# A two-layer attention and expert kernel: second route stage and second-layer attention in one stage, first stacks loaded earlier, fewer scatters between the splits

## What is computed

```
x  = x + attn0(xn) + experts0(xn)            # layer 0, xn = layernorm(x)
xn = layernorm(x)                            # layer 1
x  = x + attn1(xn) + experts1(xn)

experts1(xn):
    h = rmsnorm(xn)
    scores = softmax(h @ gate_w.T)           # 32 experts, the best 4 of each token
    w = top4 / sum(top4)
    routed: each expert takes at most 512 rows (C = 2*N/E), later ones are dropped
    shared = silu(h @ sg) * (h @ su) @ sd
    return xn + routed + shared
```

## Time and profile before

| | us |
|---|---|
| median of three runs | 1288.99 (1284.65 to 1291.62) |
| the profiled execution | 1279.91 |
| its span | 1278.1 |
| route stage of layer 1, TensorE's first matmul to its last one's end | 894.12 to 951.85 |
| attention of layer 1, TensorE's first matmul | 969.31 |
| experts of layer 1, first load | 1069.83 |

### The profile page before, as it was taken

One profiled execution on the slowest core, in us unless ns is written; L12 is line 12 of the kernel. 1 busy time (PEld: TensorE's weight loads), 2 busy tenths in 40 slices (PEclk: granted clock), 3 DMA queues, 4 the chain that ended last, 5 costly groups with the idle time before them and its releaser, 6 DMA issues. The chain is left out here.

```text
span 1278.1 us, 20689 instructions
## 1 busy us (share of the span) xinstructions
PE 1119.2 (88%) x5586; PEld 839.3 (66%) x5586; DVE 801.9 (63%) x2224; ACT 524.2 (41%) x1423; POOL 548.8 (43%) x528
## 2 busy tenths in 40 slices
PE   5659999999987999778888999995976997999981
PEld 5436667777776888555555777785544674888861
DVE  5758787666403555379999777625834664666648
ACT  2226766555502444345555555603112331444420
POOL 0656776655200000066565655404276441555540
PEclk9779999999998999989999999998997997999985
DMA  9644442222237666432222222102557932555557
GB/s 330 248 146 164 164 144 86 76 71 72 117 139 187 182 184 182 135 100 71 79 75 71 75 75 76 28 1 78 228 201 212 297 126 61 167 165 166 164 165 246
DMA packets 118684, 177.53 MB, mean 139 GB/s; under 512 B 17231, under 2 KB 86958, under 8 KB 118046
## 3 DMA queue, kind: packets, MB, share of 16 engines
q1 hardware_dynamic: 88910, 123.45, 31.0%
q0 software_dynamic: 13808, 38.19, 8.8%
q10 hardware_dynamic: 15856, 14.56, 3.3%
HBM read 103.95 MB, written 72.19 MB: 138 GB/s over the span
## 5 line engine op out<-in xcount | busy, mean ns | idle before, releaser
L907 POOL TENSOR_TENSOR parts<-wq,parts 128x256 fp32r<-128x256 f32 x64 | 48.8, 762 | 373.9 <-ACT parts L1154 373.9
L1306 PE MATMUL bank<-big_a,probsT 128*128 x760 | 202.1, 361 | 0.3 <-DVE probsT L1386 0.2
L1163 ACT ACTIVATE probs<-bank,negmax 128x256 f32<-128x256 f32 (+3 forms) x256 | 134.7, 536 | 120.1 <-DVE negmax L1078 117.9
L970 PE MATMUL bank<-kT,qT 128*128 128x256 f32 (+3 forms) x512 | 172.1, 458 | 0.0
L986 PE MATMUL bank<-const,probs 128*128 128x128 f32 x640 | 129.6, 276 | 26.2 <-DVE probs L1090 26.1
L1002 PE MATMUL bank<-probsT,big_b 128*128 128x512 f32 (+3 forms) x512 | 149.0, 434 | 0.0
L1306 PEld LDWEIGHTS bank<-big_a,probsT 128*128 128x128 f32 x760 | 131.0, 195 | 21.8 <-issue 2.7
L1078 DVE TENSOR_REDUCE negmax<-bank 128x1 f32<-128x256 f32 (+3 forms) x256 | 113.6, 485 | 47.2 <-PE bank L972 46.1
L1392 DVE TENSOR_TENSOR work<-work,bank 128x96 f32<-128x96 f32 (+1 forms) x190 | 51.4, 270 | 133.0 <-ACT work L1353 131.8
L954 PE MATMUL bank<-parts 128*128 128x512 f32 x256 | 116.9, 492 | 19.9 <-POOL parts L907 15.0
L1275 POOL DMA_INDIRECT yk_dram<-work,place x95 | 91.1, 959 | 90.4 <-DVE place L1415 53.6
(11 more groups left out here) (230 smaller groups left out, 2106.5 us busy)
## 6 DMA issues: line engine op xcount, KB each, us to landing
probs<-xs_dram SPq DMA_DIRECT2D x190, 132.0 KB
work<-khT_dram SPq DMA_DIRECT2D x64, 256.0 KB, 3.3
xs_dram<-big_a SPq DMA_DIRECT2D x16, 792.0 KB, 11.1
ys_dram<-work ACTq DMA_DIRECT2D x95, 128.0 KB, 1.7
wq<-in_wq SPq DMA_DIRECT2D x64, 128.0 KB
yk_dram<-big_a SPq DMA_DIRECT2D x16, 512.0 KB, 4.4
big_a<-yk_dram SPq DMA_DIRECT2D x32, 256.0 KB, 7.0
big_a<-in_gu SPq DMA_DIRECT2D x1, 6144.0 KB, 18.4
```

What stands on the lines that cost most here:

```text
L970: nc.tensor.matmul(s.ps[bank][:, at:at + w], s.qT[:, par, i * P:(i + 1) * P], s.kT[:, par, 0:w], start=True, stop=False)
L1163: nc.scalar.activation(s.probs[:, par, ROW_AT[i]:ROW_AT[i] + (i + 1) * P], s.ps[bank][:, at:at + (i + 1) * P], ACT.Exp, bias=s.negmax[:, p ...
L1306: mm = nc.tensor.matmul(s.ps[2 + i % 2][:, 0:W], rowsT[:, i % 2, k * P:(k + 1) * P], gu[:, k, bass.ds(e * W, W)], start=k == 0, stop=k == ...
```

## The change

The attention no longer opens a block of its own: `attention1` makes its semaphores and hands back functions for each engine, and each engine's list in `route_block` calls them at its end. The barrier between the two stages is gone; single waits on semaphores of the route stage (`joined`) stand for it. SyncE issues the first twelve stack loads and `sums` behind the high-part stores of batch 3, ahead of the low-part stores. The scatters are counted one by one: five ahead of each split, nine behind the last split, then the same 40. The dropped weights are made another way: DVE subtracts the largest logit (L720 of the new code), ScalarE takes the exponential of all 32 logits, and DVE multiplies by `over`, `many` and the reciprocal of the top four's sum, one factor after each of the first three `add_down`. TensorE asks for `sums` after scores(0) and no longer before.

```
-EARLY_TILES = 6
+SCATTERS = [(t, k) for t in range(TILES) for k in range(TOPK)]
+EARLY, BETWEEN = 15, 9
...
+            attention = attention1(nc, s, d, lambda name: sem(f"{name}_c"), joined)
...
                     sp.dma_start(stack[0, :, 1], k_hi).then_inc(stored[b % 2], 16)
                     sp.dma_start(stack[1, :, 1], k_hi).then_inc(stored[b % 2], 16)
+                    if b == BATCH - 1:
+                        attention.first_stacks(sp)
                     sp.wait_ge(low_ready, 2 * b + 2)
...
                 for i in range(2):
                     sp.wait_ge(stored[i], 16 * 6 * BATCH // 2)
-                sp.wait_ge(early_in, 32)
+                attention.sync(sp)
...
                 for b in range(1, BATCH):
-                    for t in (2 * b - 2, 2 * b - 1):
-                        scatter_tile(nc, s, d, 1, t, moved)
+                    for t, k in SCATTERS[EARLY * (b - 1) // 3:EARLY * b // 3]:
+                        scatter_tile(nc, s, d, 1, t, moved, (k,))
                     split_low(b)
-                for k in range(TOPK):
-                    pool.wait_ge(moved[k], 16 * EARLY_TILES)
+                attention.gpsimd(pool)
...
                 a(shifted_top, shifted_top, ACT.Exp).then_inc(weights_exp, 1)
+                if layer == 1:
+                    act.wait_ge(logits_shifted, 1)
+                    a(s.logits[:], s.logits[:], ACT.Exp).then_inc(logits_exp, 1)
...
+            if layer == 1:
+                v.tensor_tensor(s.logits[:], s.logits[:], top[:, :, 0:1].to_broadcast([P, TILES, EXPERTS]),
+                                ALU.subtract).then_inc(logits_shifted, 1)
...
+            factors = (over, many, rowsum.unsqueeze(2).to_broadcast([P, TILES, EXPERTS]))
+            dve.wait_ge(logits_exp, 1)
             for b in range(1, BATCH):
                 hidden(b - 1)
                 take(b)
                 add_down(b - 1)
+                if b > 1:
+                    dve.wait_ge(dropped, b - 1)
+                v.tensor_tensor(s.logits[:], s.logits[:], factors[b - 1], ALU.mult).then_inc(dropped, 1)
...
+    def first_stacks(sp):
+        sp.wait_ge(joined.projected, BATCH)
+        sp.wait_ge(joined.stored[0], 16 * 6)
+        for u in range(STACKS1):
+            load_stack(sp, u)
+        sp.dma_start(sums, d["sums1"]).then_inc(sums_in, 16)
...
+                if u == 0:
+                    pe.wait_ge(joined.x_added, {0: 2 * BATCH - 1}.get(bank, 2 * BATCH))
...
-            pe.wait_ge(sums_in, 16)
-            pe.wait_ge(ones_ready, 1)
-            scores(0)
+        pe.wait_ge(joined.taken, 4 * BATCH)
+        scores(0)
+        pe.wait_ge(sums_in, 16)
+        pe.wait_ge(ones_ready, 1)
```

More of the change, by code:

```diff
@@ L657, in _ @@
             down(BATCH - 1)
+            attention.tensor(pe)
         @block.vector
@@ new lines, in attention1, with load_stack @@
+    scored, maxed, shift_ready, producted, score_ready, exped = map(
+        sem, ("scored", "maxed", "shift", "producted", "score", "exped"))
+    weighted, head_out, summed, recip_ready, normed, wo_done, x_added = map(
+        sem, ("weighted", "head_out", "summed", "recip", "normed", "wo_done", "x_added"))
+    stack_in = [sem(f"stack_in{i}") for i in range(STACKS1)]
+    w_in, sums_in, ones_ready = sem("w_in"), sem("sums_in"), sem("ones_ready")
+    parts = Buffers()
+    def load_stack(sp, u):
+        b, h = divmod(u, H1)
+        for part in range(3):
+            sp.dma_start(s.stacks[part * HP1:(part + 1) * HP1, u % STACKS1].bitcast(F32),
+                         d["stack1"][b, part, h * HP1:(h + 1) * HP1].rearrange("l a n -> l (a n)")
+                         ).then_inc(stack_in[u % STACKS1], 16)
@@ new lines, in first_stacks, with sync @@
+    def first_stacks(sp):
[4 more added lines that the diff above has]
+        sp.dma_start(sums, d["sums1"]).then_inc(sums_in, 16)
+    def sync(sp):
+        gu, dn = d["gu1"].rearrange("(k p) n -> p k n", p=P), d["dn1"]
+        sp.wait_ge(joined.dropped, 3)
+        for u in range(NU):
+            if u < 8:
+                a = u * EARLY_GU1 // 8
+                z = a + EARLY_GU1 // 8
+                sp.dma_start(s.gu1[:, :, a:z], gu[:, :, a:z]).then_inc(w_in, 16)
+                sp.dma_start(s.gu1[:, 0, EARLY_GU1 + a:EARLY_GU1 + z], gu[:, 0, EARLY_GU1 + a:EARLY_GU1 + z]
+                             ).then_inc(w_in, 16)
+            elif u < 12:
+                a = (u - 8) * EARLY_DN1 // 4
+                z = a + EARLY_DN1 // 4
+                sp.dma_start(s.dn1[:, a:z], dn[:, a:z]).then_inc(w_in, 16)
+            if u + STACKS1 < NU:
+                sp.wait_ge(producted, u + 1)
+                load_stack(sp, u + STACKS1)
+        sp.wait_ge(w_in, 16 * 20)
+        sp.wait_ge(joined.early_in, 32)
@@ new lines, in scalar, with exps, head_of @@
+    def scalar(act):
+        def exps(u):
+            for n, (bank, tiles) in enumerate(SCORES1_T):
+                at, w = PROBS1_AT[n], sum(ROWS - j for j, _ in tiles) * P
+                act.wait_ge(score_ready, len(SCORES1_T) * u + n + 1)
+                if n == 0 and u >= 2:
+                    act.wait_ge(weighted, u - 1)
+                nc.scalar.activation(probsT[u % 2][:, at:at + w], s.ps[bank][:, 0:w], ACT.Exp).then_inc(exped, 1)
+        def head_of(u):
+            b, h = divmod(u, H1)
+            lanes = slice(h * HP1, (h + 1) * HP1)
+            act.wait_ge(weighted, u + 1)
+            if b >= 2 and h == 0:
+                act.wait_ge(wo_done, 2 * (b - 1))
+            nc.scalar.activation(heads[b % 2][lanes], HEAD_BANK[lanes, :], ACT.Copy).then_inc(head_out, 1)
+        for u in range(NU):
+            exps(u)
+            if u:
+                head_of(u - 1)
+        head_of(NU - 1)
@@ L1823 @@
+    parts.first_stacks = first_stacks
+    parts.sync, parts.gpsimd, parts.tensor, parts.vector, parts.scalar = sync, gpsimd, tensor, vector, scalar
+    return parts
 DROPPED_BANKS = (4, 5, 6, 7, 0, 1, 2, 3)
```

338 lines of the change are left out of this document (137 added, 201 removed).

## The result

The changed kernel takes 1275.32 us (median of five, 1275.17 to 1280.09) against 1288.13 (1283.91 to 1291.62) for the kernel before: ratio 0.9923, 95% interval 0.9899 to 0.9947. The forecast was 1278.8 us. Two later sets of runs gave 1273.67 against 1283.78 and 1275.50 against 1282.25.

A forecast was written before the change was run, and what follows sets the result against it. Both stages were taken as TensorE-bound, the boundary as a 17.3 us hole waiting for the `sums` load. Terms -10.6 and +0.4 (clock) gave -10.2 us: 1288.99 to 1278.8, range 1274 to 1284, widened by A and B to 1271 to 1286.

The forecast's parts named there:

- first term, -10.6: Boundary of route stage and attention: scores(1) starts at 960.5 instead of 971.11, 10.6 us earlier, subtraction's 0.53 included.
- The clock: Behind the boundary: granted clock falls to half again for 5 to 6.9 us, costing on average 0.4 us more than before.
- its holding would be worth 2.5: Boundary: if the granted clock stayed up across the hole, 2.5 us more would be gained.
- move as a block: Last twelve of 16 units, attention's end, barrier and expert stage: same instructions in the same order, so they shift together.
- VectorE's subtraction: Route stage, ahead of the one-hot chain: 0.69 us added on DVE, of which 0.53 us pass to TensorE.
- Three multiplications: DVE, after the adds of batches 0 to 2: 0.69 us each, covered by waits; bounds 0 to 1 us, taken as 0.
- GpSimd's logits operations: Eight operations from 960.39 on leave GpSimd; they held back only the first expert weights, alone worth nothing.
- The fewer scatters: GpSimd, five instead of eight between splits: last split moves from 954.01 to 948.0, worth 0 to 0.1 us.
- the 961.1: Boundary: first data at 949.5 plus stores 2.8, loads 6.3 and seven scatters at 0.35 us sharing the DMA engines.
- rival A: Boundary: transfers meet without loss (`sums` at 958.9) and the clock holds; gain 14.7 us, time 1274.3, chance 0.20.
- Rival B: Boundary: hole is DMA-bound, `sums`, last of the loads, lands near 965; gain 6 us, time 1283, chance 0.14.
- C: DMA engines, 950 to 975: scatters, stores, stack loads and expert weights meet, stacks land late; slower, 1292, chance 0.04.

The follow-up runs named there:

- set 1: First set of follow-up runs, with its own runs of the kernel before (median 1283.78 us); the changed kernel, run again unchanged, took 1273.67 us.
- weights later: Changed kernel with the attention's expert weight pieces loaded two units later: 1270.5 us, ratio to before 0.9897.
- early `sums`: Changed kernel with the load of `sums` moved to the start of the route stage, behind the two early expert loads: 1267.05 us.
- late loads: Changed kernel with the twelve stack loads and `sums` issued behind the two low-part stores of batch 3, stages still merged: 1274.07 us.
- fill: Changed kernel with unused multiplications keeping TensorE at work in the hole, 8 behind the last down projection and 18 behind scores(0): 1275.3 us.
- set 3: Third set of runs, on another chip (before: median 1282.25 us); the changed kernel, run once more, took 1275.5 us, ratio 0.9943.
- the joined variant: Changed kernel with `sums` loaded at the start of the route stage and expert weight pieces two units later, together: 1272.93 us.
- the small factors: Changed kernel with VectorE's three multiplications of the logits cut to one column of the experts: 1275.22 us, ratio 0.9943.
- the old order with `sums` first: Kernel before, stages apart, with `sums` loaded ahead of the six stacks instead of behind them: 1280.35 us against 1284.33.
- the 24 scatters: Changed kernel with 24 scatters ahead (8 behind each split as before) and none behind the last split: 1276.27 us.
- joined variant with fill: Changed kernel with early `sums` and later expert weights, plus 8 unused multiplications behind the last down projection and 3 behind scores(0): 1274.11 us.
- the wait that was to fix it: Early `sums` kernel with GpSimd's key multiplication in the first layer's attention waiting for VectorE's addition of expert rows: 1430.85 us, ratio 1.1159.

## Why the prediction was right, point by point

*Where the loads begin:* 949.87 for 949.98. *scores(0):* 954.35 for about 955. *sums:* used at 960.16 for 960.5, 10.29 us behind the first load's issue, between the bounds of 8.95 and 12.5. The rule of the Trainium skill that transfers of all issuers share the same 16 engines ("DMA: Bandwidth & Descriptors", "Issuing engines are not separate DMA queues") agrees with the trace: a share of 1.02 in 952.5 to 960.1, with q1 at 81.1% and q0 at 20.8% in 950 to 961. The prediction's first term, -10.6, measured -10.95.

*The clock:* the term that was mis-sized. +0.4 was the forecast, from a half clock of 5 to 6.9 us. It measured 12.4 us of work in after, and 13.0, 6.9, 10.2 and 11.1 in the four traces of set 1 (changed kernel, weights later, early `sums`, late loads), for 6.5 before: +0.2 to +3.25 us, in after +2.95. The stretch before was also read short, as ending at 976.2, where the row of 977 to 978 shows 977.6. That the clock would fall again was right. That its holding would be worth 2.5 no run shows: with fill it held only up to the late signals. What makes the half clock last 7 us in one trace and 13 in another is open.

*Missing:* the late signals, 3.56 us of standstill in after; no row of before shows one. The forecast named no such term. Its "move as a block" was said of the last twelve units and what follows, and it held from scores(3) on: 4.1 to 4.2 us in every unit, 4.0 at the last matmul.

*VectorE's subtraction:* 0.53 to TensorE was predicted. TensorE's place at 944 relative to that at 870 (ahead of the stage) moved by 0.35 us in after and in the four traces of set 1. *Three multiplications:* taken as 0; two are blocked to 1.45, and cut to one column they change nothing that can be measured. The reason given, that TensorE has 7 us of projection ahead of it, does not hold behind the third: after it no projection follows, and in after TensorE waited 2.08 us for 1.41 there. That moves scores(0) and not scores(1), which waits for `sums`. *GpSimd's logits operations:* taken as 0, and no run tests them alone. *The fewer scatters:* worth 0 to 0.1 us by the forecast, which saw the take of batch 3 wait for the split but followed only TensorE's projections from there. The path goes on by the high parts and their stores to the stack loads: undone, scores(1) comes 2.4 us later by the traces, while the times differ by 0.8, inside the scatter. *The transfers:* the 961.1 takes 0.35 us for a scatter where the rows read above it give about 0.4; with that it is 961.4, and nothing hangs on it.

*The sum.* -10.2 us was applied to the median and to the profile alike. The median moved by 12.8, 10.1 and 6.8 us in three sets, the profiled pair by 4.6, because the profiled execution of before was one of the quickest and that of after had late signals. For the profiled execution the forecast of 1269.7 was 5.6 us off. The time, 1275.32 by the median, came out between the forecast and rival A (1274.3), and not for A's reasons: the clock did not hold. At the boundary the traces show 4.1, 8.2 and 6.9 us where the medians of the same sets moved by 12.8, 10.1 and 6.8; before has one trace, so where its usual executions lose the rest is open. The agreement of the median with the forecast is in part luck. Rival B (`sums` near 965) and C (later stacks wait) did not occur: in 978 to 1040 TensorE is busy 62.00 of 62.00 us in after and in the four traces of set 1. B's reason was right all the same: one load of 64 KB at the end of the burst is worth 6.6 us by the medians and 5.1 at the boundary by the traces, 1.4 of that by the shorter half clock.

## What to carry to other kernels

Ask of a burst of loads which is the last that anyone waits for, and whether it must be in the burst at all: moved to the front, `sums` gave 6.6 us on top of the merge's 10.1, for two lines. When engines feed one another, follow a wait that is gone or new down to the transfers that it starts, and not only to the next busy engine: the scatters ahead of a split set when the stack loads began. A gain at a boundary is not whole until TensorE is back at full clock and its consumers are in step; read the three units behind the hole before the sum is closed. Compare medians and traces within one set only.

## What the runs showed of the hardware

**Late signals.** In six traces signals of TensorE arrived 2 to 5 us after their matmuls, and then often several within 0.1 us: after, the changed kernel of set 3, fill, the joined variant, the same with fill, and the small factors (the least, 2 us: L1709's first matmul ends at 967.70, its signal is at 969.66). Full DMA engines are not what they have in common: in after the DMA share beside them is near 1.0, in the joined variant 0.32 to 0.83 from 962 to 970 and 0.02 to 0.86 from 970 to 974. The four traces of set 1, with shares of 0.63 to 0.93 in 960 to 967, have none. What goes with them is the recording: the traces of before and of set 1 hold 20,108 to 20,157 recorded semaphore updates, all others 15,384 to 16,115. Six of the eight of these that were read for it have late signals; the old order with `sums` first and the 24 scatters have not. Whether executions without a kept trace have late signals is open; that three of six of the joined variant lie near 1271 and two near 1279.5 would fit.

**Two engines that block each other, and the executions of 20 us less.** The profiled execution of the joined variant with fill took 1252.2 us. What makes it short is not the boundary but the first layer's attention: between 568 and 712 TensorE goes from 2.5 us behind before to 21.3 ahead. VectorE's groups in 600 to 650 (count, busy us, mean ns, idle us), before and then this execution:

```profile
L1096 DVE SCALAR_TENSOR_TENSOR x_res<-big_a,weight,x_res 128x256 f32<-128x256 f32 x12 | 13.0, 1085 | 0.6
L1090 DVE TENSOR_SCALAR probs<-probs,rsum 128x384 f32<-128x384 f32 x6 | 8.5, 1417 | 0.0
```

```profile
L1113 DVE SCALAR_TENSOR_TENSOR x_res<-big_a,weight,x_res 128x256 f32<-128x256 f32 x14 | 6.7, 481 | 0.7
...
L1107 DVE TENSOR_SCALAR probs<-probs,rsum 128x384 f32<-128x384 f32 x7 | 2.9, 416 | 0.0
```

In the usual execution the addition starts at 607.66 and GpSimd's key product at 607.75, unit after unit:

```profile
607.66 2.27 DVE L1096 SCALAR_TENSOR_TENSOR x_res<-big_a,weight,x_res 128x256 f32<-128x256 f32 x2
```

```profile
607.75 1.30 POOL L920 TENSOR_TENSOR kT<-big_b,work 128x512 f32<-128x512 f32 x1
```

In the short one they lie apart, a unit takes 7.2 us for 8.8, and TensorE is busy 25.0 of 25 us for 21. The first layer is the same code in both kernels, and executions of one kernel differ by the same 20 us, so it seems that one program settles into one of two meetings and keeps it for the some fourteen units of this stretch; only one short execution has a trace. In it the meeting has moved rather than gone: the 128x128 pieces of the normalisation take 750 ns there for 274 before. The Trainium skill ("SBUF — State Buffer", "Who interferes with whom") says that VectorE with two SBUF inputs and GpSimd take turns at a shared port for whole instructions; the rows of the additions and of the multiplication, which have two such inputs, agree (1085 for 481 ns, and at the boundary 1.45 for 0.69 us). What tips the loop into one or the other is not shown, and the wait that was to fix it did not.

The best kernel measured is the changed one with `sums` loaded first: 1267.05 us against 1273.67 and 1283.78 in its set.
